# A four-expert FFN with gathered tokens: where the next expert's list, gathers and transposes stand in the hand-over between experts

## What is computed

```python
logits = flat_x @ Wg + bg                       # 2048 tokens, 4 experts
top_vals, top_idx = jax.lax.top_k(logits, 2)
...
for i in range(E):                              # E = 4
    assigned = (top_idx == i).any(axis=-1)
    score = jnp.where(assigned, probs[:, i], -jnp.inf)
    sel_p, sel_idx = jax.lax.top_k(score, capacity)      # capacity = 512
    p = jnp.where(jnp.isfinite(sel_p), sel_p, 0.0)[:, None]
    tok = flat_x[sel_idx]
    h = jax.nn.gelu(tok @ W1[i], approximate=False)      # 512 -> 2048
    y = h @ W2[i] * p                                    # 2048 -> 512
    out = out.at[sel_idx].add(y)
```

## Time and profile before

| | us |
|---|---|
| median of 3 runs | 493.35 (493.11 to 493.76) |
| the profiled execution | 493.46 |
| its span, first to last instruction | 491.7 |
| PE busy | 417.2 (85% of the span) |
| PEld, DVE, ACT, POOL busy | 202.6, 316.1, 252.6, 115.1 |
| mean granted TensorE clock over the span | 0.943 |
| expert changes begin (list on TensorE) | 185.30, 270.33, 355.36 |

### The profile page before, as it was taken

How to read it: one execution, slowest core, us unless ns; L and a number is a source line. 1 busy time by engine, 2 the same in 40 slices (tenths; PEclk the granted TensorE clock), 3 DMA queues, 4 the chain that set the end, 5 groups by cost and what they waited for, 6 DMA issues and landing times.

```text
span 491.7 us, 7201 instructions
## 1 busy us (share of the span) xinstructions
PE 417.2 (85%) x2032; PEld 202.6 (41%) x2032; DVE 316.1 (64%) x608; ACT 252.6 (51%) x382; POOL 115.1 (23%) x128
## 2 busy tenths in 40 slices
PE   2568677810189999999999999999999999999992
PEld 2334333400055444444444444444444444444440
DVE  7989999788739995292788238278723737771000
ACT  6547588966525555861544685155469424440000
POOL 0857746661031003132000312100040210001111
PEclk9988999965579999999999999999999999999998
DMA  7893011399121704829100844800093310000311
GB/s 263 322 385 129 9 72 49 122 295 401 58 87 48 295 0 170 279 36 350 21 1 0 311 139 131 267 7 0 1 339 108 40 26 0 0 0 1 42 23 21
DMA packets 23126, 59.62 MB, mean 121 GB/s; under 512 B 1280, under 2 KB 1408, under 8 KB 21056
## 3 DMA queue, kind: packets, MB, share of 16 engines
q1 hardware_dynamic: 19008, 50.15, 27.5%
q0 software_dynamic: 3664, 8.65, 8.6%
q10 hardware_dynamic: 432, 0.54, 0.3%
HBM read 46.76 MB, written 12.58 MB: 121 GB/s over the span
## 4 chain that ended last, share of the span: by engine, by line
PE 72%; DVE 19%; issue 3%; ACT 3%; POOL 1%; ACTq 0%; DVEq 0%; POOLq 0%
PE ps L713 34%; PE ps L698 32%; DVE arena L1095 6%; PE ps L659 2%; DVE arena L1114 2%; DVE bn L1080 2%; DVE arena L1125 2%; DVE arena L1328 2%; PE ps L630 1%; PE ps L636 1%; ACT rows L795 1%; PE ps L651 0%; DVE arena L1383 0%; PE ps L590 0%; DVE spot L1337 0%
## 5 line engine op out<-in xcount | busy, mean ns | idle before, releaser
L713 PE MATMUL ps<-arena 128*128 128x512 f16 x768 | 167.4, 379 | 0.0
L698 PE MATMUL ps<-arena,early 128*128 128x512 f16 x720 | 156.1, 379 | 0.0
L713 PEld LDWEIGHTS ps<-arena 128*128 128x128 f16 x768 | 74.9, 98 | 88.6
L698 PEld LDWEIGHTS ps<-arena,early 128*128 x720 | 70.4, 98 | 85.0
L902 ACT ACTIVATE arena<-ps,up 128x512 f32<-128x512 f32 x64 | 44.0, 687 | 82.1 <-PE ps L698 73.0
L1035 POOL DMA_INDIRECT result<-arena,idx x16 | 28.1, 1755 | 156.6 <-DVE arena L1454 142.3
L1454 DVE TENSOR_SCALAR arena<-ps,yscale 128x512 f32<-128x512 f32 x16 | 12.0, 748 | 78.6 <-PE ps L713 57.9
L897 ACT ACTIVATE arena<-rows,down x64 | 45.6, 712 | 30.1 <-PE ps L713 30.1
L1439 DVE SCALAR_TENSOR_TENSOR arena<-arena,h_down 128x512 f32 x64 | 48.1, 752 | 9.7 <-DVE arena L1437 0.8
L1414 DVE SCALAR_TENSOR_TENSOR early<-w_raw,down,early 128x2048 f16<-128x2048 f32 x16 | 36.8, 2343 | 22.3 <-ACT early L860 22.3
L1026 POOL DMA_INDIRECT arena<-xn_table,idx x16 | 16.8, 1047 | 141.4 <-DVE plist L1397 137.7
(11 more groups left out here) (172 smaller groups left out, 386.2 us busy)
## 6 DMA issues: line engine op xcount, KB each, us to landing
w_raw<-in_L_ffn_W SPq DMA_DIRECT2D x4, 4096.0 KB, 14.2
rows<-in_L_ffn_W SPq DMA_DIRECT2D x3, 4096.0 KB, 16.3
rows<-in_L_ffn_W SPq DMA_DIRECT2D x4, 1024.0 KB, 11.1
result<-rows SPq DMA_DIRECT2D x3, 1024.0 KB, 6.9
early<-in_ctx SPq DMA_DIRECT2D x2, 1024.0 KB, 6.6
rows<-in_x SPq DMA_DIRECT2D x2, 1024.0 KB, 11.7
xn_table<-arena SPq DMA_DIRECT2D x4, 512.0 KB, 3.6
xn_table<-arena SPq DMA_DIRECT2D x2, 1024.0 KB, 7.6
```

The source lines that it names most:

```text
L698: last = nc.tensor.matmul(ps[:, PH[q], :], w[:, k, at], t[:, k, :], start=n == 0, stop=n == 3 * CT - 1)
L713: last = nc.tensor.matmul(ps[:, PY[s % 2], :], h[:, t, s * P:(s + 1) * P], w[:, t, :], start=t == 0 and n == 0, stop=t == HT - 1 and n == 2)
```

## The change

TensorE adds up the next list behind down block 1 in place of ahead of down block 0, and transposes all four token blocks behind down block 2, in place of two behind block 1 and two behind block 2. The four blocks have four PSUM banks (4 to 7) in place of two, and the waits between them go. VectorE takes the list behind `h_scales`, then does `take_y(e, 1)`, `w1_low` 0 and 1, `take_y(e, 2)`, all of `token_low`, `w1_low` 2 and 3. ScalarE does two of the W2 magnitudes, all of `token_high`, then the other two magnitudes. GpSimd does the scatter of down block 0 and the all-reduce for W1 before the four gathers, and the scatters of blocks 1 and 2 behind them.

```diff
--- before.py
+++ after.py
@@ -273,7 +273,7 @@
         PR = [5, 6] * (TT // 2 - 1) + [3, 0]
         PC, PW, PF, PG, PI = 7, 4, 5, 6, 4
         PT_L = 1
-        PH, PY, PT, PT0 = [0, 1, 6, 7], [2, 3], [4, 5], [2, 3, 4, 5]
+        PH, PY, PT, PT0 = [0, 1, 6, 7], [2, 3], [4, 5, 6, 7], [2, 3, 4, 5]
 
 
         s_cst = sem("constants_landed")
@@ -616,18 +616,14 @@
                 last.then_inc(b_hotused, 1)
 
 
-            def tokens(done, blocks):
+            def tokens(done):
 
                 for s in range(ST):
                     pe.wait_ge(c_tok[s], (done + 1) * 16)
                 pe.wait_ge(b_taken, done * 2 + 2)
-                for k in blocks:
-
-                    if k >= 2:
-                        pe.wait_ge(c_tokhi, START + done * CT + k - 1)
-                        pe.wait_ge(c_toklo, START + done * CT + k - 1)
+                for k in range(CT):
                     for s in range(ST):
-                        last = nc.tensor.transpose(ps[:, PT[k % 2], s * P:(s + 1) * P], tok[:, s, k * P:(k + 1) * P], ident)
+                        last = nc.tensor.transpose(ps[:, PT[k], s * P:(s + 1) * P], tok[:, s, k * P:(k + 1) * P], ident)
                     last.then_inc(c_tokt, 1)
 
             def keep_warm(count):
@@ -716,12 +712,11 @@
 
             def next_expert(e):
 
-                next_list(e)
                 down_block(e, 0)
                 down_block(e, 1)
-                tokens(e + 1, (0, 1))
+                next_list(e)
                 down_block(e, 2)
-                tokens(e + 1, (2, 3))
+                tokens(e + 1)
                 down_block(e, 3)
 
             first_tokens()
@@ -881,10 +876,10 @@
                     nc.scalar.activation(spent[:, k % 2, :], some, ACT.Abs, scale=1.0 / (HT * D // CT),
                                          accum_out=wmax[:, 1, k:k + 1]).then_inc(c_w2sum, 1)
 
-            def token_high(done, blocks, bank=PT * 2):
-                for k in blocks:
+            def token_high(done):
+                for k in range(CT):
                     act.wait_ge(c_tokt, START + done * CT + k + 1)
-                    nc.scalar.copy(tok_hi[:, k, :], ps[:, bank[k], :]).then_inc(c_tokhi, 1)
+                    nc.scalar.copy(tok_hi[:, k, :], ps[:, PT[k], :]).then_inc(c_tokhi, 1)
 
             def gelu_and_w2(e):
 
@@ -918,9 +913,9 @@
                 act.wait_ge(c_h, START + (e + 1) * HT)
                 w1_magnitudes(e + 1)
                 w1_high(e + 1)
-                token_high(e + 1, (0, 1))
-                w2_magnitudes(e + 1)
-                token_high(e + 1, (2, 3))
+                w2_magnitudes(e + 1, (0, 1))
+                token_high(e + 1)
+                w2_magnitudes(e + 1, (2, 3))
             gelu_and_w2(E - 1)
 
 
@@ -1058,9 +1053,10 @@
             pool.wait_ge(c_first, 1)
             for e in range(E - 1):
                 pool.wait_ge(c_tokt, START + (e + 1) * CT)
+                scatter(e, [0])
+                share_top(2 * e + 3, 0)
                 gather(e + 1)
-                share_top(2 * e + 3, 0)
-                scatter(e, [0, 1, 2])
+                scatter(e, [1, 2])
                 share_top(2 * e + 4, 1)
                 scatter(e, [3])
                 added(e)
@@ -1414,10 +1410,10 @@
                     nc.vector.scalar_tensor_tensor(w1_lo[:, :, some], w1_raw[:, :, some], down[:, 0:1], w1_hi[:, :, some],
                                                    ALU.mult, ALU.subtract).then_inc(c_w1lo, 1)
 
-            def token_low(done, blocks, bank=PT * 2):
-                for k in blocks:
+            def token_low(done):
+                for k in range(CT):
                     dve.wait_ge(c_tokhi, START + done * CT + k + 1)
-                    nc.vector.tensor_tensor(tok_lo[:, k, :], ps[:, bank[k], :], tok_hi[:, k, :], ALU.subtract).then_inc(c_toklo, 1)
+                    nc.vector.tensor_tensor(tok_lo[:, k, :], ps[:, PT[k], :], tok_hi[:, k, :], ALU.subtract).then_inc(c_toklo, 1)
 
             def halves_of_h_and_w2(e, first, last):
 
@@ -1469,18 +1465,17 @@
                 halves_of_h_and_w2(e, 0, 2)
                 slots(e + 1)
                 halves_of_h_and_w2(e, 2, HT // HB)
-                take_list(e + 1)
                 row_scale(e)
                 take_y(e, 0)
                 w1_top(e + 1)
                 power_scale(e * 2 + 3, 0)
                 h_scales(e + 1)
+                take_list(e + 1)
+                take_y(e, 1)
                 w1_low(e + 1, (0, 1))
-                take_y(e, 1)
-                token_low(e + 1, (0, 1))
+                take_y(e, 2)
+                token_low(e + 1)
                 w1_low(e + 1, (2, 3))
-                take_y(e, 2)
-                token_low(e + 1, (2, 3))
                 w2_top(e + 1)
                 power_scale(e * 2 + 4, 1)
                 take_y(e, 3)
```

## The result

| | before | changed |
|---|---|---|
| median, us | 493.36 (6 runs, 493.04 to 493.76) | 496.0 (6 runs, 495.68 to 496.24) |
| span of the profiled execution, us | 491.7 | 493.9 |
| PE busy, us | 417.2 | 417.4 |

The account below looks back on a forecast made before the run. TensorE's back-to-back work was taken to bound the kernel. Other terms cost 0; a 1.0 us gap at each of three expert changes adds 3.0 us to the 493.35 us median: 496.4 us, range 493.2 to 500.6.

Parts of the forecast that it names:

- What bounds the kernel: From 154 to 482 us TensorE's own work bounds it; a change can only open gaps, at three expert changes.
- The undisturbed chain fits: At an expert change, list, four unheld gathers and landing finish before TensorE wants the transposes, with 1.2 us to spare.
- The holds: Second and third gathers wait for the running w1_low to end; gap 1.0 us a change, 3.0 us; chance 0.57.
- The number 0.11 us: Fitted time after an indirect DMA's start when it needs something unavailable until the running VectorE instruction ends.
- When w1_low starts: VectorE's first w1_low starts 2.1 us behind the list, at 208.12 at the first change.
- the time from the fourth gather's start to the transposes: On GpSimd's fourth gather: it lands 3.5 us after its start, and TensorE takes up the landed rows 0.2 us later.
- The first gather's margin: At the first change the first gather asks 0.26 us ahead of w1_low, so it runs free.
- all held: Rival: first gather, too late, is held too; gap 2.3 us a change, 7.0 us in all, 500.4 us; chance 0.20.
- The covers: Work behind the transposes (token_low, w1_low 2 and 3, W2 scales, scatters, W1 load) is ready before wanted; cost 0.
- Locks both ways: Rival: a running gather shuts out w1_low for its whole length; 8.1 us, 501.5 us; chance 0.03, shared with unseen later wait.

## Why the prediction was right

**What bounds the kernel:** right. PE busy is 417.2 and 417.4 us, and the difference is idle time at the three places that were named.

**The undisturbed chain fits:** right. It was said to leave 1.2 us. With w1_low out of the way the transposes start on time in all three changes. There the fourth gather starts at 211.39; with the 3.66 to 3.90 us that the changed kernel took from there to the transposes, they could begin at 215.1 to 215.3, 1.1 to 1.3 us before TensorE is free at 216.37 (an estimate from these rows). In the kernel with eight short instructions a hold of 0.43 us was swallowed.

**The holds:** right, from scatters carried over to gathers. Forecast for the first change were gathers of 1.0, 2.3, 1.9 and 1.0 us; measured 1.13, 2.38, 1.96 and 1.01. The number 0.11 us, fitted to two scatters, gave every held gather of the changed kernel and of the experiments within 0.05 us, on top of the free 1.01 us (1.11 for the first of four). The step that was only supposed, that it is the second SBUF input that counts, was shown by the run with one input from PSUM. That it is the read of the index list that is held is still an inference: no run changed where the list is read.

**When w1_low starts:** 2.1 us behind the list was forecast for all three changes. Measured are 2.30, 1.92 and 1.92. At the first it waits for ScalarE's high halves, which come 0.2 us later than worked out; at the others these are ready and VectorE itself is the limit, with take_list and take_y 1. This term was a little off in both directions. The other term that was off is the time from the fourth gather's start to the transposes: 3.5 + 0.2 + 0.22 = 3.92 us was forecast, 3.66, 3.90 and 3.80 were measured. At the first change the later w1_low and the quicker landing cancel, and that the gap is 1.00 us to the hundredth is luck. At the others both terms, the start of w1_low above all, make the gap smaller: 0.87 and 0.76. The sum was forecast as 3.0 and is 2.63.

**The first gather's margin:** forecast 0.26 us (the terms given, 206.57 + 1.12 + 0.11, make it 0.32); measured 207.72 - 207.25 = 0.47 at the first change, and 293.41 - 293.34 = 0.07 at the second. The rival "all held" was thus nearer than it was thought to be: a cast 0.45 us later brought it about at two changes of three.

**The price of "all held"** was put at 7.0 us. The waiting was sized rightly (2.1 to 2.3 us a gap), but the clock's share was left out: 505.5 us was measured with three such gaps, not 500.4. I had taken the clock as given, since it is 1.00 over the stretch of the earlier trace rows. The upper end of the range was too low for that case.

**The covers** behind the transposes held: in no run with the gap away does TensorE wait for a half, a scale or a landed scatter. Token_low ended 3.7 to 3.8 us behind the start of the transposes where 3.2 was said, well within its cover.

**"Locks both ways"** is refuted: in the changed kernel w1_low starts at 207.72 under a gather that runs from 207.14 to 208.27, and the w1_low pair lasts 4.60 to 4.62 us with gathers let in beside it, as long as without.

The Trainium skill (page "SBUF — State Buffer", section "Who interferes with whom") says that a VectorE instruction with at most one SBUF input, outside of two modes of its own, doesn't contend with GpSimd, and one with two does if the GpSimd instruction reads SBUF. The runs agree with both halves: 1.01 to 1.13 us against 1.44 to 4.59. The page's rule (section "SBUF: two separate sides") that whichever starts first keeps the port pair for its whole instruction is not borne out for an indirect DMA that starts first: w1_low beside it was not held (4.62 us for the pair).

## What to carry to other kernels

When an indirect DMA is moved, look at what VectorE runs at the new place: instructions with two SBUF inputs hold each of a row of indirect DMAs to their own end, so what counts is not VectorE's load but the length of its single instructions and how many boundaries fall among the issues. Short instructions, one operand in PSUM, or the same work moved behind the gathers each took the whole cost away here. And where a tensor-bound kernel waits for several transfers, let it wait for each in turn ahead of the work on that one: the last lateness then hides behind the work on the rest.

## What the runs showed of the hardware

- An indirect DMA of 128 rows that asks (0.11 us after its start) under a VectorE instruction with two SBUF inputs stands until that instruction ends: gathers of 1.01 us became 1.44 to 4.59 us. It gets in between two such instructions that follow each other without a pause, and doesn't lengthen them.
- With one of VectorE's inputs from PSUM, gathers beside it took 1.01 to 1.13 us, as long as with no such instruction beside them.
- In the profiled executions, gaps of TensorE of 1.87 us and less left its granted clock at 1.00 (2.4 GHz). Behind gaps of 2.09 to 2.30 us it fell; the mean over the transposes was 0.55 to 0.82, where 0.5 would be the 1.2 GHz level throughout, and it was back at 1.00 within the next down block. In the kernel with one long w1_low that cost 1.7 us a time, three quarters of what the gap itself did, though less in one of its four executions. Ten products that computed nothing, put into the gap, gave it back.
